# Block 0's first K rows from spread weights, x normalised in place, and new orders of five instruction streams

## The reference

```python
q, k, v = x @ Wq, x @ Wk, x @ Wv            # 16 heads of 8
fg = sigmoid(x @ Wf + bf)
state = state * fg[..., None] + v[..., None] * k[..., None, :]   # per token
out = einsum('bhij,bhj->bhi', state, q)
out = layernorm(out) * gamma + beta
att = (out * silu(x @ Wg)) @ Wout
x = layernorm(x + att)
h = silu(x @ w1.T * s1) * (x @ w2.T * s2)    # 512 hidden
h = gelu(h @ h1.T * t1); h = gelu(h @ h2.T * t2)
x = layernorm(x + h @ w3.T * s3)
```

## Time and profile before

| | us |
|---|---|
| runs (three) | 510.16, 510.31, 510.43 |
| median | 510.31 |
| profiled execution | 509.54 |
| its span, first to last instruction | 507.7 |
| TensorE busy | 495.2 |
| VectorE busy | 447.1 |
| ScalarE busy | 405.7 |
| POOL busy | 309.9 |

### The profile page before, as it was taken

How to read it: one execution, slowest core, us unless ns; L and a number is a source line. 1 busy time by engine, 2 the same in 40 slices (tenths; PEclk the granted TensorE clock), 3 DMA queues, 4 the chain that set the end, 5 groups by cost and what they waited for, 6 DMA issues and landing times.

```text
span 507.7 us, 8095 instructions
## 1 busy us (share of the span) xinstructions
PE 495.2 (98%) x2528; PEld 383.5 (76%) x2528; DVE 447.1 (88%) x708; ACT 405.7 (80%) x839; POOL 309.9 (61%) x362
## 2 busy tenths in 40 slices
PE   8999999999999999999999999999999999999995
PEld 6667787877878786777877777787867777787994
DVE  4999899999999998999899999899999999992351
ACT  5677788887897878878898787889788788878873
POOL 1832839487492939758393876748385775928322
PEclk9999999999999999999999999999999999999999
DMA  7999999718089976698896871770996790600001
GB/s 260 229 240 236 217 216 220 194 51 192 0 207 220 248 177 134 155 225 196 186 234 175 195 202 26 200 170 1 217 212 131 173 220 25 156 31 1 22 23 44
DMA packets 43372, 79.47 MB, mean 157 GB/s; under 512 B 4928, under 2 KB 5952, under 8 KB 43072
## 3 DMA queue, kind: packets, MB, share of 16 engines
q1 hardware_dynamic: 43040, 78.61, 63.6%
q10 hardware_dynamic: 288, 0.33, 0.2%
HBM read 11.81 MB, written 4.19 MB: 32 GB/s over the span
## 4 chain that ended last, share of the span: by engine, by line
PE 69%; issue 8%; DVE 8%; POOL 8%; ACT 3%; SPq 2%; DMA 1%; POOLq 0%; ACTq 0%; DVEq 0%
PE F L2301 41%; PE back L2402 8%; PE front L2202 6%; DVE KJ L1557 3%; PE back L2287 2%; POOL h1lo L441 2%; PE back L2186 2%; PE ps_v L2202 2%; POOL h2lo L441 2%; PE back L2269 2%; SPq L283 2%; POOL KJ L502 1%; PE F L2198 1%; DMA QJ<-qk 1%; DVE h L1621 1%
## 5 line engine op out<-in xcount | busy, mean ns | idle before, releaser
L441 POOL TENSOR_TENSOR h1lo<-h,h1hi 128x512 fp32r<-128x512 f32 x60 | 76.6, 1293 | 18.5 <-ACT h1hi L864 18.0
L871 ACT ACTIVATE h<-F,cols 128x512 f32<-128x512 f32 x120 | 80.5, 686 | 8.6 <-PE F L2301 7.6
L441 POOL TENSOR_TENSOR h2lo<-h,h2hi 128x512 fp32r<-128x512 f32 x60 | 76.1, 1291 | 10.5 <-ACT h2hi L864 10.4
L1557 DVE TENSOR_TENSOR_SCAN KJ<-g,carry,KJ 128x512 f32<-128x512 f32 x64 | 78.3, 1264 | 0.4 <-ACT g L803 0.2
L1557 DVE TENSOR_TENSOR_SCAN KJ<-g,KJ 128x512 f32<-128x512 f32 x64 | 74.2, 1202 | 0.4 <-ACT g L803 0.3
L508 POOL TENSOR_TENSOR QJ<-QJ 128x512 f32<-128x512 f32 x14 | 18.0, 1284 | 91.5 <-DVE QJ L1572 91.5
L2301 PE MATMUL F<-h2hi,whi 128*128 128x512 f32 (+1 forms) x256 | 72.1, 417 | 0.6 <-ACT h L871 0.5
L1564 DVE TENSOR_TENSOR QJ<-QJ,KJ 128x1024 f32<-128x1024 f32 x60 | 71.3, 1212 | 1.0 <-DMA QJ<-qk 0.8
L2301 PE MATMUL F<-h1hi,whi 128*128 128x512 f32 (+1 forms) x256 | 70.7, 414 | 1.0 <-DVE h L1621 0.8
L2301 PE MATMUL F<-h1lo,whi 128*128 128x512 f32 (+1 forms) x256 | 67.7, 401 | 0.4 <-POOL h1lo L441 0.4
L2301 PE MATMUL F<-h2lo,whi 128*128 128x512 f32 (+1 forms) x256 | 66.4, 402 | 0.0
(11 more groups left out here) (182 smaller groups left out, 937.7 us busy)
## 6 DMA issues: line engine op xcount, KB each, us to landing
KJ<-qk SPq DMA_DIRECT2D x120, 256.0 KB, 4.8
QJ<-qk SPq DMA_DIRECT2D x120, 256.0 KB, 4.8
x_in<-in_x SPq DMA_DIRECT2D x16, 256.0 KB, 4.8
xT<-in_xT SPq DMA_DIRECT2D x15, 256.0 KB, 4.9
out<-res SPq DMA_DIRECT2D x15, 256.0 KB, 2.0
wraw<-in_wffn SPq DMA_DIRECT2D x2, 1024.0 KB, 8.7
wraw<-in_wffn SPq DMA_DIRECT2D x2, 256.0 KB, 4.5
wproj<-in_wproj SPq DMA_DIRECT2D x2, 192.0 KB, 3.6
```

The source lines that it names most:

```text
L441: e.tensor_tensor(h_lo[layer][:, t, :w], h[:, t, :w], h_hi[layer][:, t, :w].bitcast(f32), ALU.subtract).then_inc(lo_done[layer], 1)
L871: e.activation(dst[:, t, :WIDTH[n]], F[t][:, :WIDTH[n]], ACT.Gelu, scale=scale[t]).then_inc(gelu_done[layer], 1)
L1557: e.tensor_tensor_scan(K, g[:, :WIDTH[n]], K, init, ALU.mult, ALU.add).then_inc(scan_done, 1)
```

## The change

Four things change. (1) For block 0, K's rows 0 and 1 are projected directly: `make_spread(j)` copies column j of each head of Wk eight times, once for each i, and a plain projection by it gives the spread row. v and f are projected first. (2) `norm_o` writes into `y`, `norm_1` into `x_in` itself; the buffers `o_norm` and `x1` are gone, x_in has three buffers, and a load of x waits for the square of the block that used the buffer. (3) The transfers have another order, among others the last weights ahead of x(0). (4) The five streams have other orders, most in blocks 0 to 5 and some up to block 15; the tables FREED and XT_READ follow. The number of instructions stays the same, but for two copies more on VectorE and two matmuls less on TensorE.

```diff
-    XB, XTB, GB = 2, 4, 3
-    SLOTS = 2
+    XB, XTB, GB = 3, 4, 3
+    SLOTS, SPREAD = 2, 2
...
+        k_spread = sb("k_spread", [P, SPREAD, D])
...
-        o_norm = sb("o_norm", [P, NC_ * D])
         y = sb("y", [P, T])
-        x1 = [sb(f"x1_{p}", [P, NC_ * D]) for p in range(2)]
...
+        def spread(j):
+            return k_spread[:, j, :]
...
             def load_x(n):
                 if n >= XB:
-                    e.wait_ge(norm_done["1"], n - XB + 1)
-                    if n == XB:
-                        e.wait_ge(half_done["1"], 1)
+                    e.wait_ge(squared, n - XB + 1)
...
@@ sync: the first transfers
             load_xT(2)
+            load_xT(3)
+            fetch(1, 1, 0)
+            fetch(1, 1, 1)
             load_w3()
-            fetch(1, 1, 0)
-            load_xT(3)
-            fetch(1, 1, 1)
+            load_weights(3)
             fetch(1, 0, 0)
             load_x(0)
-            load_weights(3)
             fetch(1, 0, 1)
-            load_xT(4)
-            fetch(2, 1, 0)
             load_x(2)
             load_x(1)
+            fetch(2, 1, 0)
+            load_xT(4)
...
             load_xT(15)
+            load_x(11)
+            load_x(12)
             fetch(12, 0, 1)
-            load_x(11)
...
@@ gpsimd: the first operations
+            kvj_gp(2)
             qsj_gp(0)
-            kvj_gp(2)
             kvj_gp(4)
...
@@ scalar
             def norm_o(n):
                 if n:
-                    e.wait_ge(yT_made, n)
-                normalise(n, "o", o_norm, lambda c: o_chunk(n, c))
+                    e.wait_ge(att_made, n)
+                normalise(n, "o", y, lambda c: o_chunk(n, c))
...
             def norm_1(n):
-                if n == 1:
-                    e.wait_ge(w3_averaged, 1)
-                elif n:
-                    e.wait_ge(squared, n - 1)
-                normalise(n, "1", x1[n % 2], lambda c: x_in[n % XB][:, chunk(c)])
+                normalise(n, "1", x_in[n % XB], lambda c: x_in[n % XB][:, chunk(c)])
...
             halve_bias()
-            hi_0(0)
-            hi_0(1)
             copy_v(0)
             tanh(0)
             g_of_tanh(0)
+            sum_low_parts(0)
+            hi_0(0)
+            hi_0(1)
             copy_k(1)
...
             affine(0)
-            sum_low_parts(2)
+            sum_low_parts(3)
+            tanh(3)
+            split_weights(2)
+            split_weights(3)
+            norm_1(0)
+            silu_gate(2)
+            g_of_tanh(2)
+            x1_hi(0)
+            silu(0, 0)
+            save_carry(1)
             copy_q(2)
+            silu(0, 1)
+            copy_q(3)
             copy_v(2)
-            split_weights(2)
-            sum_low_parts(3)
-            norm_1(0)
-            x1_hi(0)
-            silu_gate(2)
-            silu(0, 0)
-            silu(0, 1)
-            split_weights(3)
...
             hi(1, 0, 3)
+            center_w3()
+            copy_k(4)
             norm_o(1)
...
@@ vector
+            def make_spread(j):
+                e.wait_ge(wproj_landed[0], 16)
+                src = WK.rearrange("p (h j) -> p j h", j=HD)[:, j, :]
+                e.tensor_copy(spread(j).rearrange("p (h i) -> p h i", i=HD), src.unsqueeze(2).broadcast_to([P, P // HD, HD])).then_inc(spread_done, 1)
...
@@ tensor
             def project_kj(j):
                 freed("kj", j)
+                if j < SPREAD:
+                    e.wait_ge(spread_done, j + 1)
+                    project(0, (front, ps_v)[j % 2], spread(j)).then_inc(kj_made, 1)
+                    return
                 select(0, j, (front, ps_v)[j % 2]).then_inc(kj_made, 1)
...
@@ block 13 and block 14
                 mid_lo(1, 13, 3, low_parts)
+                project_gate(15)
                 mid_open(2, 13, 2, low_parts)
...
                 up_lo(14, 3, low_parts)
-                project_gate(15)
                 mid_open(1, 14, 0, low_parts)
...
@@ the head
+            project_v(0)
+            project_f(0)
+            project_kj(0)
             project_0(0)
             project_0(1)
-            project_v(0)
-            project_kj(0)
-            project_f(0)
+            project_k(1)
             project_kj(1)
-            project_k(1)
```

More of the change, by code:

```diff
@@ L409, in _ @@
             fetch(13, 0, 0)
+            fetch(13, 0, 1)
             fetch(14, 1, 0)
-            load_x(12)
             fetch(14, 1, 1)
-            fetch(13, 0, 1)
+            load_x(13)
             fetch(15, 1, 0)
-            load_x(13)
             fetch(14, 0, 0)
@@ L1028, in _ @@
             gelu(2, 0, 3)
-            save_carry(2)
+            copy_q(4)
+            copy_v(3)
             silu(1, 0)
@@ L1035, in _ @@
             silu(1, 2)
+            save_carry(2)
             silu(1, 3)
+            g_of_tanh(3)
             hi(1, 1, 1)
             hi(1, 1, 2)
+            norm_o(2)
             hi(1, 1, 3)
-            norm_o(2)
             affine(2)
@@ L1067, in _ @@
             hi(1, 2, 2)
+            norm_2(0)
+            hi(1, 2, 3)
+            save_carry(3)
+            square(1)
             silu_gate(4)
-            square(1)
-            g_of_tanh(4)
-            hi(1, 2, 3)
-            copy_k(5)
             norm_o(3)
@@ L1161, in _ @@
             copy_k(8)
+            hi(1, 5, 1)
             silu(5, 2)
-            hi(1, 5, 1)
+            g_of_tanh(7)
+            silu_gate(7)
+            save_carry(6)
             silu(5, 3)
-            silu_gate(7)
+            norm_o(6)
+            copy_q(8)
             hi(1, 5, 2)
-            save_carry(6)
-            norm_o(6)
+            square(4)
             hi(1, 5, 3)
             affine(6)
-            copy_q(8)
+            tanh(8)
             gelu(1, 5, 0)
             hi(2, 5, 0)
-            square(4)
-            tanh(8)
             gelu(1, 5, 1)
+            hi(2, 5, 1)
             gelu(1, 5, 2)
-            hi(2, 5, 1)
             gelu(1, 5, 3)
-            norm_1(6)
             hi(2, 5, 2)
             hi(2, 5, 3)
+            norm_1(6)
             norm_2(3)
             x1_hi(6)
+            gelu(2, 5, 0)
+            copy_v(8)
+            gelu(2, 5, 1)
             g_of_tanh(8)
-            gelu(2, 5, 0)
-            gelu(2, 5, 1)
             copy_k(9)
@@ L1190, in _ @@
             gelu(2, 5, 3)
-            copy_v(8)
+            save_carry(7)
             silu(6, 0)
@@ L1200, in _ @@
             hi(1, 6, 2)
+            square(5)
+            norm_o(7)
             hi(1, 6, 3)
-            save_carry(7)
-            norm_o(7)
-            square(5)
             affine(7)
@@ L1221, in _ @@
             gelu(2, 6, 3)
+            save_carry(8)
             silu(7, 0)
-            tanh(9)
+            g_of_tanh(9)
             copy_v(9)
+            silu(7, 1)
             hi(1, 7, 0)
-            save_carry(8)
-            silu(7, 1)
+            hi(1, 7, 1)
             silu(7, 2)
-            hi(1, 7, 1)
             silu_gate(9)
@@ L1279, in _ @@
             hi(2, 8, 3)
+            copy_q(12)
             copy_v(11)
-            copy_q(12)
-            square(7)
             norm_1(9)
@@ L1346, in _ @@
             copy_k(13)
+            save_carry(11)
+            norm_2(8)
             hi(2, 10, 3)
@@ L1393, in _ @@
             hi(1, 12, 1)
+            silu(12, 2)
+            g_of_tanh(14)
             copy_q(14)
-            silu(12, 2)
             silu(12, 3)
-            square(11)
+            silu_gate(14)
             hi(1, 12, 2)
@@ L1409, in _ @@
             hi(2, 12, 1)
+            tanh(15)
             hi(2, 12, 2)
@@ L1417, in _ @@
             gelu(2, 12, 3)
+            square(11)
             silu(13, 0)
+            silu(13, 1)
             copy_v(15)
-            silu(13, 1)
             hi(1, 13, 0)
             hi(1, 13, 1)
+            square(12)
+            save_carry(14)
             silu(13, 2)
-            tanh(15)
             silu(13, 3)
-            save_carry(14)
             g_of_tanh(15)
             hi(1, 13, 2)
+            copy_q(15)
+            norm_o(14)
             hi(1, 13, 3)
-            norm_o(14)
-            copy_q(15)
             affine(14)
@@ L1439, in _ @@
             gelu(1, 13, 3)
-            square(12)
             hi(2, 13, 3)
```

751 lines of the change are left out of this document (370 added, 381 removed).

## The result

The changed kernel takes 511.53 us (median of 22 runs, 508.37 to 514.88), the kernel before, run beside it, 510.14 (22 runs, 509.21 to 511.24): ratio 1.0034, interval 1.0021 to 1.0047. I had forecast 509.9, no difference. The profiled execution took 513.07, its span 511.2.

What follows compares the result with a forecast made beforehand. Bound: a 43.17 us head, then TensorE's work with 3.6 us of holes, then 6.3 us of stores. Head -0.5, other orders +0.1: -0.4 on 509.54, 509.1; with 0.77 to the median, 509.9 us; 8-in-10 range 508.0 to 511.2.

Steps and rivals of the forecast that it cites:

- 2. The weights' last part ahead of x(0): SyncE's queue, head: 1 MB (4.4 us) ahead of x(0), issued at 24.15; lands near 33.4, needed at 35.8, hidden by 2.4.
- in the middle blocks: Sign of being wrong: VectorE waits for a transfer in the blocks after the head; no size given.
- 1. Spread weights, f first: Head, K's row 0 by one projection, spread copy 0.2 us: first scan at 8.2 instead of 10.18, 2.0 us earlier.
- What eats those 2 us: VectorE, head: work moved behind the first scan; second scan about 11.5, 1.1 us earlier; stats_o(0) at 27.1, 0.7 later.
- From stats_o(0) to x1: Head: gated_y0 about 33.8, residual_1(0) 35.8; x1's statistics about 0.2 us earlier, norm_1(0) about 39.45, transposes 40.65.
- Behind the transposes: TensorE, head: up_hi(0, 0) at 42.45, 0.7 us earlier; project_q(3) waits for copy_q(2); 0.5 us of gain left.
- 3. In place: norm_o writes y, norm_1 writes x_in: nothing on the path; tightest place found is load_x(12), hidden by 3 us.
- 4. Other orders: TensorE, blocks 13 and 14: project_gate(15) fills the 0.54 hole, the 0.33 hole grows by up to 0.87; net +0.1 us.
- my 3 to 5: Sign expected: TensorE's holes from 43 to 501 us sum to 3 to 5 us.
- Rival B: TensorE behind the head: new orders also close half of the 3.6 us of holes, about 508.0 us; chance 0.28.
- D: Slower: ScalarE centres w3 before norm_o(1); if it ends behind 58.2, TensorE waits 1.5 us; at 59, 512; chance 0.13.
- E: VectorE, head: four scans behind the first each wait out a POOL product of 1.26: 5 us, 514.8; chance 0.02.

## Why the prediction was wrong

**The step that failed is "2. The weights' last part ahead of x(0)"**: "lands near 33.4: hidden by 2.4". It landed at 38.6. Three things were wrong in it.
- The start, 28.8 (24.15 + 4.6), was right, and so was the price of 1 MB in bytes: 4.4 us, and 9.0 - 4.6 = 4.4 in the run that moved it alone. But I kept the issue at 24.15. It came at 26.85 there: most of the difference is the time that SyncE spends on issuing the transfer (2.26 us in that profile). So this transfer costs the one behind it twice, in the issuing queue and on the way; w3 and its scale, alone in the kernel before, cost it only in the queue.
- I counted one of the transfers put ahead. w3 and its scale stand there too. Putting them back, with the weights still ahead, brought x(0) 2.7 us earlier (35.9 for 38.6), and it is they that used up the last of the cover: with the weights alone ahead, the changed kernel has no wait, by 0.1 to 0.4 us.
- By bytes the 320 kB are 1.4 us. The scale, read 128 times from one row, gave 1.5 us alone, in single profiles. Its price hangs on what is issued behind it, see the last section.

The Trainium skill (DMA: Bandwidth & Descriptors, "Queues, rings and completion order") says that on each DMA engine descriptors are consumed in ring order; by that rule x(0) has to wait for the bytes ahead, and the trace agrees: 4.6, 9.0 and 11.2 us to landing.

**What it cost.** None of my rivals had a late transfer in the head or a fall of the clock; among the signs that I would be wrong, only waits for transfers "in the middle blocks" stood. Instead of being hidden by 2.4 us, x(0) kept VectorE waiting 2.03. Against the kernel before, up_hi(0, 0) starts 2.7 us later and up_hi(0, 2) 3.5 (49.83 for 46.38; with x(0) first it starts at 46.25). The moves of the transfers alone cost the old kernel 5.3 us, and moving x(0) ahead of all of them, or w3 and its scale back, took the loss away. The clock is part of that, and by the two halves of the runs it seems to have fallen in about half of them: in the profile of the changed kernel 2.25 us pass from the transposes to up_hi(0, 0), with w3 back 1.47. The Trainium skill (TensorE: Matmul & The Clock Gate, "HAM oscillation — how this bites in real kernels") describes a TensorE that falls to its low clock because it waits for transfers; the trace agrees, with 0.58 and 0.57 behind the idle of 2.15 us.

**1. Spread weights, f first**: right. 8.18, 11.54; the spread copy took 0.22, I had 0.2. In some profiles the first projection takes about twice as long and all of the head is 1 us later, see below. **What eats those 2 us** and **From stats_o(0) to x1**: right within 0.1.

**Behind the transposes**: the wait for copy_q(2) is there, 0.44 and not 0.7; the branch costs from nothing to 1.06 where I had 0.3. Where it costs nothing the kernel gains more than my 0.4: the three kernels with w3 back stand at 0.9980 to 0.9982, 0.9 to 1.0 us below before, all their intervals below 1. How much of that is the head's their profiles don't show: their first projection was slow, and up_hi(0, 2) stands at 46.41 to 46.75, no earlier than before.

**3. In place**: right for the changed kernel's profile, where no engine waited on a load of x behind block 0. But load_x(12), hidden by 3 us, was not the tightest place. With the new order x(4) is issued at 148.77, lands in 4.0 and is used at 153.48: 0.7 us of cover, where the kernel before issued it at 95.47. In two of the experiments it came too late, and TensorE idled 0.78 and 1.32 us; how many of their runs, or of the changed kernel's, have this wait is not known.

**4. Other orders**: the hole of 0.54 was filled, the one of 0.33 grew by 0.85; +0.3, the upper end of my range, for +0.1. All holes together 4.31, inside my 3 to 5. Rival B (holes close) did not come, nor D: norm_o(1) ended at 60.35 us, in a head 3.5 us later (at 56.77 with x(0) first, where I expected 56.3), and TensorE shows no hole behind it. Nor E: the second scan takes 1.22, as before.

## What to carry to other kernels

When a transfer moves ahead of another, list every transfer that moves with it, and allow for the one behind both the issue time on the queue and the time on the way; then compare with the first user, and with the first user of the transfer that moved back. Do it for each later load whose place changed, x(4) here, and not for one alone. Where a late input would leave TensorE idle, reckon the wait and a stretch at the low clock.

## What was not expected of the hardware

- The first 128x512 projection has no fixed duration: 0.86 us to the next start in the kernel with x(0) first, 1.70 in the changed kernel's profile, and values between in others (1.04, 1.25, 1.61), behind the same warm-up products. The rows' granted clock is 1.00 in that stretch in both, so they don't show why. VectorE's first scan comes at 8.18 or 9.27 with it, residual_1(0) at 35.74 or, ready, at 36.66.
- While the scale's load was on its way, the traffic of the changed kernel broke down. From the view of the transfers between 20 and 30 us, GB/s in slices of 0.25 us:

```profile
GB/s 262 197 205 180 205 197 188 205 188 221 229 320 270 232 172 127 158 111 53 12 115 121 35 233 201 231 133 131 166 266 362 297 395 414 279 369 377 336 246 148
```

From 23.75 to 25.75 us it is 12 to 158, where some 200 are usual, and the scale takes 7.4 us to landing. It is not the scale by itself. Where the 1 MB is issued right behind it, it took 6.4 to 7.5 us in seven profiles, each with such a fall. With the 1 MB behind x(0) it took 3.9 us in the changed kernel and 4.6 in the kernel before, and no slice of 0.25 us while it was on its way is under 156 GB/s. What the two do to each other is not shown.
